# A windowed-attention block on one core: make_k and project ahead of turn 1, make_q and center2 ahead of attend 0, with two small moves beside it

## The chip, the cores and the metric

The program runs on one core of one Trainium2 chip. The time is the device time of an execution in microseconds (us), lower is better. The five engines are TensorE (PE), VectorE (DVE), ScalarE (ACT), GpSimd (POOL) and SyncE (SP, which here only moves data). Each works through its own list of instructions in order, and they meet only at semaphores.

## The reference, cut to what matters

One Swin block on x of shape (4, 32, 64, 64): windows of 8 x 8 positions, 4 heads of 8 channels, all in float32.

```python
xw = windows(x)                                     # (4*64, 64, 32)
h = layernorm(xw, ln1_g, ln1_b)
q, k, v = split(h @ qkv_w.T + qkv_b)                # 4 heads of 8
attn = softmax((q * 8 ** -0.5) @ k.T + bias)        # 64 x 64 for each window and head
o = (attn @ v) @ proj_w.T + proj_b
xw = xw + o
h = gelu(layernorm(xw, ln2_g, ln2_b) @ fc1_w.T + fc1_b)
out = xw + h @ fc2_w.T + fc2_b
```

## The kernel before

The 128 partitions hold the 4 images' 32 channels. The picture is cut into 8 stripes of 8 rows (512 positions, 8 windows for each image). Every engine's program is a loop over c = 0 to 9; pass c, called body c here, works on three stripes at once: the attention of stripe c, the first layernorm and q, k, v of stripe f = c + 1, and projection, residual and second layernorm of stripe p = c - 1. What comes first on an engine is fixed by the order of calls in that loop, written out by hand; no scheduler changes it. After the attention bodies the two MLP products of all stripes follow.

The attention of a stripe goes in two halves t = 0, 1 of four units each (a unit g is one image's 4 windows of that half), with these steps:

- PE `score(c, t)` (L678): q times masked k into the four PSUM banks S_PS[0..3], one for each image.
- DVE `add_bias` (L485) copies a bank with the bias added into s_sb, and `find_max` (L495) takes the row maximum; POOL `subtract_max` (L215) subtracts it.
- PE `turn(c, r)` (L694), r = 0 to 3, transposes two units into the banks T_PS[0] and T_PS[1]; ACT `exp_round(c, r)` (L260) takes the exponential into pt. Turn r + 1 waits until exp r has read the banks.
- PE `attend(c, t)` multiplies pt by v (L712) and by ones for the denominators (L719). For t = 0 both go to S_PS[1]. ACT `inv_den(c, t)` makes the inverse by Ln (L321) and Exp (L323), and DVE `divide(c, t)` (L515) multiplies it in. The next stripe's score writes all four banks and so waits for divide(c, 0), among four other semaphores.

For the next stripe: PE `center1` (L610), ACT `square1` (L267), PE `variance1` (L628), ACT `inv_std1` (L273, L275), DVE `norm1` (L503), then PE `make_k` and `make_q` (L604) and `make_v` (L653), and ACT `copy_k` (L285, with the head-masked copies at L290), `copy_q` (L298) and `copy_v` (L313); POOL `mask_keys` (L207) makes the other two masked copies. For the stripe before: PE `project` (L610), DVE `residual` (L521), PE `center2` (L610), DVE `keep2` (L526), ACT `square2` (L329), PE `variance2` (L604), ACT `log_var2` and `inv_std2` (L335, L339), POOL `norm2` (L221). project, center2 and variance2 all use the bank Y_PS. PE takes pairs of them together (make_k with project, make_q with center2, variance2 with center1), since they use different quarters of the array; their waits stand ahead of the pair.

The listings of the order below are of one engine each, without repeats of the same instruction.

## Time and profile before

| | us |
|---|---|
| median of 3 runs | 177.25 (176.6 to 177.63) |
| the profiled execution's own time | 178.3 |
| its span, first to last instruction | 176.6 |
| PE busy | 156.7 |
| ACT busy | 128.2 |
| DVE busy | 118.9 |
| POOL busy | 91.1 |

The span is what the trace shows; the rest of the execution's time lies around it. Body 0 begins at 15.73, body 7 at 124.65, and the MLP stage, with the largest part of the output transfers, runs from about 147 to the end. A busy engine is not yet the bound: what counts is which wait ends last in a stage.

### The profile page before, as it was taken

What the parts mean: (1) busy time and instruction counts of PE and PEld (TensorE: products, weight loads), DVE (VectorE), ACT (ScalarE), POOL (GpSimd) and SP (SyncE); (2) the same over time, 40 slices, a digit from 0 to 9 for tenths busy, and PEclk for the clock granted to TensorE, in tenths of its full rate; (3) what the DMA queues carried; (4) which work ended last, traced back from release to release, by engine and by line L of the source; (5) the groups of instructions that cost most, each with busy time, mean ns of one, the idle gap of its engine ahead of it and who ended that gap; (6) DMA issues with size and microseconds to landing.
All of it is one profiled execution on the core that took longest, in us unless ns stands there. A gap on an engine that the chain in (4) does not pass through costs nothing.

```text
span 176.6 us, 6351 instructions
## 1 busy us (share of the span) xinstructions
PE 156.7 (89%) x2688; PEld 86.7 (49%) x2688; DVE 118.9 (67%) x220; ACT 128.2 (73%) x180; POOL 91.1 (52%) x103
## 2 busy tenths in 40 slices
PE   7978699999999999999999999999999794749972
PEld 7535354764575556457555754664575350111210
DVE  4556996969777896979597787969788702303332
ACT  4344967759697798769687977878683459788991
POOL 7500658638584947657585848668587420020000
PEclk9999999999999999999999999999999999988999
DMA  2760000000000000000000000000000000101333
GB/s 75 222 206 0 4 2 4 4 0 4 6 4 0 4 0 4 6 2 4 4 4 0 4 4 2 4 4 4 2 4 4 0 4 0 59 0 59 123 119 119
DMA packets 3245, 4.71 MB, mean 27 GB/s; under 512 B 946, under 2 KB 1298, under 8 KB 3218
## 3 DMA queue, kind: packets, MB, share of 16 engines
q1 hardware_dynamic: 2840, 4.23, 7.1%
q8 instruction: 21, 0.34, 0.8%
q0 software_dynamic: 256, 0.07, 0.3%
q14 instruction: 6, 0.05, 0.1%
q10 hardware_dynamic: 122, 0.01, 0.1%
HBM read 2.21 MB, written 2.10 MB: 24 GB/s over the span
## 4 chain that ended last, share of the span: by engine, by line
PE 57%; ACT 26%; DVE 7%; issue 7%; ACTq 1%; POOLq 1%; DVEq 0%
PE ps L694 14%; ACT pt L260 11%; PE ps L604 9%; PE ps L712 7%; PE ps L678 7%; PE ps L719 5%; ACT hid L350 4%; DVE s_sb L485 4%; ACT v_blk L313 3%; PE ps L757 3%; PE ps L771 3%; PE ps L653 3%; PE ps L586 2%; ACT rstd L339 2%; PE ps L610 2%
## 5 line engine op out<-in xcount | busy, mean ns | idle before, releaser
L215 POOL TENSOR_TENSOR s_sb<-s_sb,mx 128x512 f32<-128x512 f32 x64 | 66.1, 1042 | 46.9 <-DVE mx L495 46.9
L485 DVE TENSOR_TENSOR s_sb<-ps,bias_t 128x512 f32<-128x512 f32 x64 | 43.7, 683 | 12.4 <-PE ps L678 12.4
L495 DVE TENSOR_REDUCE mx<-s_sb 128x8 f32<-128x512 f32 x64 | 43.9, 686 | 2.2
L260 ACT ACTIVATE pt<-ps 128x1024 f32<-128x1024 f32 x32 | 32.7, 1021 | 12.9 <-PE ps L694 12.7
L694 PEld LDWEIGHTS ps<-ident,s_sb 128*128 128x128 f32 x256 | 27.4, 140 | 22.5 <-issue 20.7
L694 PE MATMUL ps<-ident,s_sb 128*128 128x128 f32 x256 | 35.2, 279 | 2.1 <-ACT pt L260 1.4
L678 PE MATMUL ps<-k_m,q_sb 32*64 32x256 f32 x512 | 18.5, 386 | 2.4 <-DVE att L515 1.4
L712 PEld LDWEIGHTS ps<-pt,v_blk 128*32 128x32 f32 x1024 | 15.2, 110 | 9.7 <-ACT pt L260 9.2
L712 PE MATMUL ps<-pt,v_blk 128*32 128x64 f32 x1024 | 17.8, 221 | 1.3 <-ACT pt L260 0.3
L610 PE MATMUL ps<-x_sb,cent_m 64*64 64x512 f32 x64 | 18.0, 640 | 0.9 <-DVE x_sb L521 0.9
L350 ACT ACTIVATE hid<-ps,fb 128x512 f32<-128x512 f32 (+1 forms) x16 | 16.8, 1110 | 1.8 <-PE ps L757 1.8
L604 PE MATMUL ps<-h,wqk 64*64 64x512 f32 x64 | 17.0, 613 | 0.9 <-DVE h L503 0.9
L561 DVE SCALAR_TENSOR_TENSOR y_sb<-ps,vec,x_sb 128x512 f32<-128x512 f32 (+1 forms) x9 | 6.2, 691 | 16.9 <-PE ps L771 16.9
L221 POOL TENSOR_TENSOR h_sb<-h_sb,rstd 128x512 f32<-128x512 f32 x8 | 10.2, 1275 | 13.4 <-ACT rstd L339 13.4
L719 PE MATMUL ps<-pt,ones_h 128*32 128x256 f32 x256 | 16.8, 379 | 0.0
L515 DVE TENSOR_TENSOR att<-ps,den 128x256 f32<-128x256 f32 x16 | 6.7, 420 | 14.6 <-ACT den L323 14.6
L678 PEld LDWEIGHTS ps<-k_m,q_sb 32*64 32x64 f32 x512 | 10.6, 131 | 6.1 <-ACT q_sb L298 2.8
L757 PE MATMUL ps<-h_sb,f_s 32*128 32x512 f32 x64 | 9.9, 686 | 2.4 <-POOL h_sb L221 2.4
L207 POOL TENSOR_SCALAR k_m<-k_sb,hmask 128x512 f32<-128x512 f32 x14 | 9.5, 692 | 3.7 <-ACT k_sb L285 3.7
L653 PEld LDWEIGHTS ps<-wv,h 128*64 128x64 f32 x256 | 8.1, 138 | 5.7 <-issue 3.1
L771 PE MATMUL ps<-hid,f_st 128*32 128x512 f32 (+1 forms) x72 | 9.4, 607 | 1.6 <-ACT hid L350 1.6
L604 PE MATMUL ps<-sq,mean_m 64*64 64x512 f32 x32 | 8.6, 613 | 2.2 <-ACT sq L329 2.1
(92 smaller groups left out, 180.2 us busy)
## 6 DMA issues: line engine op xcount, KB each, us to landing
x_sb<-in_x_dram SPq DMA_DIRECT2D x8, 256.0 KB, 4.9
out_dram<-y_sb SPq DMA_DIRECT2D x7, 256.0 KB, 2.0
out_dram<-y_sb SPq DMA_DIRECT2D x2, 128.0 KB, 1.8
raw_b<-in_L_conv_rpb_dram POOLq DMA_DIRECT2D x8, 8.0 KB, 2.8
f_nat<-in_L_conv_fc_w_dram SPq DMA_DIRECT2D x2, 16.0 KB
w_nat<-in_L_conv_qkv_w_dram ACTq DMA_DIRECT2D x1, 12.0 KB
p_nat<-in_L_conv_proj_w_dram SPq DMA_DIRECT2D x1, 4.0 KB
vec_r<-in_L_conv_ln_g_dram ACTq DMA_DIRECT2D x1, 0.1 KB
```

The costliest lines, as they stand in the source:

```text
L215: pool.tensor_tensor(tile, tile, mx[:, n % 4, :].unsqueeze(2).to_broadcast([128, 2 * NH, NT]), ALU.subtract).then_inc(shifted, 1)
L260: act.activation(pt[:, n % 8:n % 8 + 2, :, :, :].rearrange("p u a k n -> p (u a k n)"), ps[:, 4:6, :].rearrange("p u n -> p (u n)"), ACT.E ...
L350: act.activation(hid[:, c % 2, images, :].rearrange("p g n -> p (g n)"), ps[:, banks, :].rearrange("p g n -> p (g n)"), ACT.Gelu, bias=fb1 ...
L485: dve.tensor_tensor(s_sb[:, n % NSB, :, :, :].rearrange("p a h m -> p a (h m)"), S_PS[g].rearrange("p (a k) -> p a k", a=2), bias_t[:, :, ...
L495: dve.reduce_max(mx[:, n % 4, :], s_sb[:, n % NSB, :, :, :].rearrange("p a h m -> p (a h) m"), AX.X)\
L604: ins = pe.matmul(out[r:r + 64, :], w[r:r + 64, r:r + 64], rhs[r:r + 64, :], start=True, stop=True, tile_position=(r, r))
L610: ins = pe.matmul(out[64 - r:128 - r, :], w[r:r + 64, r:r + 64], rhs[r:r + 64, :], start=True, stop=True, tile_position=(r, 64 - r))
L678: ins = pe.matmul(S_PS[g][NT * ab:NT * (ab + 1), 256 * pr:256 * (pr + 1)], q_sb[C * g:C * (g + 1), c % 2, NT * w:NT * (w + 1)], k_m[C * g: ...
L694: ins = pe.transpose(T_PS[u][:, 128 * i:128 * (i + 1)], s_sb[:, n % NSB, pr, 2 * hp:2 * hp + 2, :].rearrange("p h m -> p (h m)"), ident[:, :])
L712: ins = pe.matmul(OD_PS[t][C * g:C * (g + 1), NT * wl:NT * (wl + 1)], v_blk[:, c % 2, G * (4 * t + wl) + g, 32 * (1 - hp):32 * (2 - hp)], ...
L719: ins = pe.matmul(OD_PS[t][C * g:C * (g + 1), 256:512], ones_h[:, hp, :], pt[:, (4 * t + g) % 8, :, hp, :], start=(hp == 0), stop=(hp == 1 ...
L757: ins = pe.matmul(ps[:, first_bank(c) + g, :], f1_s[C * g:C * (g + 1), :], h2_sb[C * g:C * (g + 1), c, :], start=True, stop=True, tile_pos ...
```

## The change

Four things move.

1. PE: make_k and project, which stood behind turn 1, stand ahead of it, and attend 0, which stood ahead of make_q and center2, stands behind them. The same instructions are issued.
2. ACT: copy_k is split. Its plain copy stands between exp 0 and exp 1; the two head-masked copies, now `scale_k`, come after exp 1, then copy_q, and inv_den(c, 0) after that, where it stood ahead of copy_q.
3. DVE: residual comes after the first unit of the second half instead of after the second, and divide(c, 0) stands ahead of the last find_max instead of behind it.
4. First values: the v product of stripe 0 goes to T_PS[0] instead of S_PS[0] and no longer waits for the first variance; the first score waits for that variance's Ln instead of for the copy of v, and the first turn waits for the copy of v.

```diff
--- before.py
+++ after.py
@@ -283,6 +283,8 @@
                 if f >= 1:
                     act.wait_ge(k_masked, f)
                 act.activation(k_sb[:, :], X_PS, ACT.Identity, bias=bq[:, 1:2]).then_inc(k_copied, 1)
+
+            def scale_k(f):
                 if f >= 2:
                     act.wait_ge(scored, 8 * (f - 1))
                 if f >= 1:
@@ -309,7 +311,7 @@
 
                     dst = v_blk[r, f % 2, :, 16:48].rearrange("p w (k e) -> p w k e", e=16)
                     dst = dst[:, :, ::-1, HD * hh:HD * (hh + 1)]
-                    src = S_PS[1 if f else 0][r].rearrange("p (w k d) -> p w k d", k=2, d=HD)
+                    src = (S_PS[1] if f else T_PS[0])[r].rearrange("p (w k d) -> p w k d", k=2, d=HD)
                     ins = act.activation(dst, src, ACT.Copy)
                 ins.then_inc(v_copied, 1)
 
@@ -375,16 +377,18 @@
                     act.preload_act_table_set("natural_log_exp_and_others")
                 if there(c):
                     exp_round(c, 0)
-                    exp_round(c, 1)
                 if there(f):
                     copy_k(f)
                     if f == 0:
                         copy_q(f)
                         copy_v(f)
                 if there(c):
+                    exp_round(c, 1)
+                if f >= 1 and there(f):
+                    scale_k(f)
+                    copy_q(f)
+                if there(c):
                     inv_den(c, 0)
-                if f >= 1 and there(f):
-                    copy_q(f)
                 if there(p):
                     square2(p)
                 if there(c):
@@ -538,16 +542,18 @@
                 if there(p):
                     divide(p, 1)
                 if there(c):
-                    for g in range(2):
-                        add_bias(c, 1, g)
-                        find_max(c, 1, g)
+                    add_bias(c, 1, 0)
+                    find_max(c, 1, 0)
                 if there(p):
                     residual(p)
                 if there(c):
-                    for g in range(2, G):
-                        add_bias(c, 1, g)
-                        find_max(c, 1, g)
+                    add_bias(c, 1, 1)
+                    find_max(c, 1, 1)
+                    add_bias(c, 1, 2)
+                    find_max(c, 1, 2)
+                    add_bias(c, 1, 3)
                     divide(c, 0)
+                    find_max(c, 1, 3)
                 if there(p):
                     keep2(p)
                 if c == -1:
@@ -646,11 +652,9 @@
             def make_v(f):
                 if f >= 1:
                     pe.wait_ge(biased, unit_of(f, 0, 1) + 1)
-                else:
-                    pe.wait_ge(log1, 1)
                 for w in range(NW):
                     for hh in range(2):
-                        ins = pe.matmul(S_PS[1 if f else 0][NT * hh:NT * (hh + 1), NT * w:NT * (w + 1)], h1[:, f % 2, w, :],
+                        ins = pe.matmul((S_PS[1] if f else T_PS[0])[NT * hh:NT * (hh + 1), NT * w:NT * (w + 1)], h1[:, f % 2, w, :],
                                         wv[:, hh, :, :].rearrange("p k d -> p (k d)"), start=True, stop=True,
                                         tile_position=(0, NT * hh))
                 ins.then_inc(v_ready, 1)
@@ -663,7 +667,7 @@
                         pe.wait_ge(k_scaled, c)
                         pe.wait_ge(divided, 2 * (c - 1) + 1)
                     else:
-                        pe.wait_ge(v_copied, 1)
+                        pe.wait_ge(log1, 1)
                 else:
                     pe.wait_ge(v_copied, c + 1)
                     if there(c + 1):
@@ -688,6 +692,8 @@
                     pe.wait_ge(shifted, n + 1)
                     if n >= 2:
                         pe.wait_ge(expd, n - 1)
+                    else:
+                        pe.wait_ge(v_copied, 1)
                     for pr in range(2):
                         for hp in range(2):
                             i = 2 * pr + hp
@@ -812,17 +818,16 @@
                 if there(c):
                     turn(c, 0)
                     score(c, 1)
+                if there(f):
+                    wait_k(f)
+                if there(p):
+                    wait_project(p)
+                if there(f):
+                    make_k(f)
+                if there(p):
+                    project(p)
+                if there(c):
                     turn(c, 1)
-                if there(f):
-                    wait_k(f)
-                if there(p):
-                    wait_project(p)
-                if there(f):
-                    make_k(f)
-                if there(p):
-                    project(p)
-                if there(c):
-                    attend(c, 0)
                 if there(f):
                     wait_q(f)
                 if there(p):
@@ -834,6 +839,7 @@
                 if p == NCH - 1:
                     down(0, 4, slice(0, TC))
                 if there(c):
+                    attend(c, 0)
                     turn(c, 2)
 
             up(1)
```

PE, one body from its second score on (body 1), before:

```order
L678 MATMUL ps<-k_m,q_sb 64x256 x16
L694 MATMUL ps<-ident,s_sb 128x128 x8
L604 MATMUL ps<-h1,wqk 64x512 x2
L610 MATMUL ps<-att,wp 64x512 x2
L712 MATMUL ps<-pt,v_blk 32x64 x32
L719 MATMUL ps<-pt,ones_h 32x256 x8
L604 MATMUL ps<-h1,wqk 64x512 x2
L610 MATMUL ps<-x1_sb,cent_m 64x512 x2
L694 MATMUL ps<-ident,s_sb 128x128 x8
L678 MATMUL ps<-k_m,q_sb 64x256 x16
L604 MATMUL ps<-sq2,mean_m 64x512 x2
```

and now (L610 is make_k, make_q and variance2, L616 project, center2 and center1, L700 the turn, L718 and L725 attend, L682 the score):

```order
L682 MATMUL ps<-k_m,q_sb 64x256 x16
L610 MATMUL ps<-h1,wqk 64x512 x2
L616 MATMUL ps<-att,wp 64x512 x2
L700 MATMUL ps<-ident,s_sb 128x128 x8
L610 MATMUL ps<-h1,wqk 64x512 x2
L616 MATMUL ps<-x1_sb,cent_m 64x512 x2
L718 MATMUL ps<-pt,v_blk 32x64 x32
L725 MATMUL ps<-pt,ones_h 32x256 x8
L700 MATMUL ps<-ident,s_sb 128x128 x8
L682 MATMUL ps<-k_m,q_sb 64x256 x16
L610 MATMUL ps<-sq2,mean_m 64x512 x2
```

Between attend's products and the next score there is now a turn alone, where make_q, center2 and the turn stood.

DVE, the same body from the first add_bias of its second half, before (L485 add_bias, L495 find_max, L521 residual, L515 divide, L526 keep2):

```order
L485 TENSOR_TENSOR s_sb<-ps,bias_t 128x512
L495 TENSOR_REDUCE mx<-s_sb 128x8
L485 TENSOR_TENSOR s_sb<-ps,bias_t 128x512
L495 TENSOR_REDUCE mx<-s_sb 128x8
L521 SCALAR_TENSOR_TENSOR x1_sb<-ps,bq,x_sb 128x512
L485 TENSOR_TENSOR s_sb<-ps,bias_t 128x512
L495 TENSOR_REDUCE mx<-s_sb 128x8
L485 TENSOR_TENSOR s_sb<-ps,bias_t 128x512
L495 TENSOR_REDUCE mx<-s_sb 128x8
L515 TENSOR_TENSOR att<-ps,den 128x4x8x8
L526 COPY h2_sb<-ps 128x512
```

and now (L489, L499, L525, L519, L530 in the same order):

```order
L489 TENSOR_TENSOR s_sb<-ps,bias_t 128x512
L499 TENSOR_REDUCE mx<-s_sb 128x8
L525 SCALAR_TENSOR_TENSOR x1_sb<-ps,bq,x_sb 128x512
L489 TENSOR_TENSOR s_sb<-ps,bias_t 128x512
L499 TENSOR_REDUCE mx<-s_sb 128x8
L489 TENSOR_TENSOR s_sb<-ps,bias_t 128x512
L499 TENSOR_REDUCE mx<-s_sb 128x8
L489 TENSOR_TENSOR s_sb<-ps,bias_t 128x512
L519 TENSOR_TENSOR att<-ps,den 128x4x8x8
L499 TENSOR_REDUCE mx<-s_sb 128x8
L530 COPY h2_sb<-ps 128x512
```

The residual moved up by one pair; the divide moved ahead of the last find_max, so that find_max and keep2 stand behind it.

## Rows read from the trace of the kernel before

**Rows 1.** Page, part 1: busy us, share of the span, instructions of each engine.
```profile
PE 156.7 (89%) x2688; PEld 86.7 (49%) x2688; DVE 118.9 (67%) x220; ACT 128.2 (73%) x180; POOL 91.1 (52%) x103
```

**Rows 2.** Five bodies as one stretch: length, busy us (instructions) of PE, PEld, DVE, ACT, POOL, granted clock, DMA share, GB/s.
```profile
44.98:124.65 79.67, 76.72 (x1571) 46.85 (x1571) 65.36 (x106) 64.15 (x100) 54.10 (x56) 1.00 0.01 3
```

**Rows 3.** Timeline of PE: start, us, operation, count, idle before and its releaser.
```profile
95.02 1.09 PE L694 MATMUL ps<-ident,s_sb 128*128 128x128 f32 x8
...
100.90 1.12 PE L678 MATMUL ps<-k_m,q_sb 32*64 32x256 f32 x32
102.22 1.07 PE L694 MATMUL ps<-ident,s_sb 128*128 128x128 f32 x8 [0.21 <-ACT pt L260]
103.22 0.65 PE L604 MATMUL ps<-h,wqk 64*64 64x512 f32 x2
...
104.45 1.10 PE L712 MATMUL ps<-pt,v_blk 128*32 128x64 f32 x64
...
106.35 0.65 PE L604 MATMUL ps<-h,wqk 64*64 64x512 f32 x2
...
107.37 1.09 PE L694 MATMUL ps<-ident,s_sb 128*128 128x128 f32 x8
108.69 1.33 PE L678 MATMUL ps<-k_m,q_sb 32*64 32x256 f32 x32 [0.23 <-DVE att L515]
```

**Rows 4.** Timeline of DVE, the same body.
```profile
101.20 0.42 DVE L515 TENSOR_TENSOR att<-ps,den 128x256 f32<-128x256 f32 x1 [1.22 <-ACT den L323]
102.08 0.69 DVE L485 TENSOR_TENSOR s_sb<-ps,bias_t 128x512 f32<-128x512 f32 x1 [0.45 <-PE ps L678]
...
104.72 0.74 DVE L521 SCALAR_TENSOR_TENSOR x_sb<-ps,bq,x_sb 128x512 f32<-128x512 f32 x1
...
107.42 0.69 DVE L495 TENSOR_REDUCE mx<-s_sb 128x8 f32<-128x512 f32 x1
108.02 0.41 DVE L515 TENSOR_TENSOR att<-ps,den 128x256 f32<-128x256 f32 x1
108.35 0.68 DVE L526 COPY h_sb<-ps 128x512 f32<-128x512 f32 x1
```

**Rows 5.** Opening: timeline of PE, then of DVE.
```profile
14.58 0.38 PE L600 MATMUL ps<-vec,f_t 32*128 32x1 f32 x2
15.73 1.12 PE L678 MATMUL ps<-k_m,q_sb 32*64 32x256 f32 x32 [0.77 <-ACT v_blk L313]
...
13.23 1.68 DVE L465 TENSOR_SCALAR k_m<-k_sb,hmask 128x512 f32<-128x512 f32 x4 [0.26 <-ACT k_sb L285]
```

**Rows 6.** Bodies 0 and 1: timeline of DVE, then of PE.
```profile
22.25 0.68 DVE L503 TENSOR_TENSOR h<-ps,rstd 128x512 f32<-128x512 f32 x1
...
29.26 1.12 PE L678 MATMUL ps<-k_m,q_sb 32*64 32x256 f32 x32
...
37.19 1.12 PE L678 MATMUL ps<-k_m,q_sb 32*64 32x256 f32 x32
```

**Rows 7.** Timeline of ACT, the body of rows 3.
```profile
100.68 0.42 ACT L323 ACTIVATE den<-den 128x256 f32<-128x256 f32 x1
101.05 1.02 ACT L260 ACTIVATE pt<-ps 128x1024 f32<-128x1024 f32 x1
103.37 1.02 ACT L260 ACTIVATE pt<-ps 128x1024 f32<-128x1024 f32 x1 [1.29 <-PE ps L694]
...
106.48 0.38 ACT L321 ACTIVATE den<-ps 128x256 f32<-128x256 f32 x1
106.90 0.42 ACT L323 ACTIVATE den<-den 128x256 f32<-128x256 f32 x1
...
109.06 0.63 ACT L329 ACTIVATE sq<-h_sb 128x512 f32<-128x512 f32 x1 [0.90 <-DVE h_sb L526]
109.60 1.01 ACT L260 ACTIVATE pt<-ps 128x1024 f32<-128x1024 f32 x1
```

**Rows 8.** Timeline of PE behind the last body.
```profile
140.74 1.08 PE L604 MATMUL ps<-sq,mean_m 64*64 64x512 f32 x4 [1.30 <-ACT sq L329]
```

More of the change, by code:

```diff
@@ L814, in _ @@
                     score(c, 1)
-                    turn(c, 1)
                 if there(f):
@@ L824, in _ @@
                 if there(c):
-                    attend(c, 0)
+                    turn(c, 1)
                 if there(f):
```

## The prediction

> **What bounds the kernel now.** I read the page first. TensorE (PE) is busy 156.7 of 176.6 us, 89%, where ScalarE (ACT) and VectorE (DVE) have 128.2 and 118.9 [rows 1]. The stretch of five whole bodies, 44.98 to 124.65, takes 79.67 us, 15.93 us a body, of which PE is busy 76.72, 15.34 a body, at clock 1.00 [rows 2]. So a body is bound by PE's list of work, and about 0.6 us of it is waits. The timeline of one body tells which. PE idles 0.21 us before turn 1 of stripe c, because exp 0 ends late. It waits before attend 0 too: make_k and project start at 103.22 and take as long as make_q and center2 do (106.35 to 107.37, 1.02), so they would be through at 104.24, and attend starts at 104.45, after exp 1 (103.37 + 1.02). It idles 0.23 before score 0 of the next stripe, released by the divide, which starts at 108.02 [rows 3, 4, 7]. (A PE row's end lies 0.07 to 0.09 beyond the start of the next, as 102.22 + 1.07 against 103.22; steps below go from start to start.) The three ask for different things: the first two for other work in front of them, the third for an earlier divide.
>
> **Opening.** The first score, at 15.73, sat idle 0.77 us for the copy of v, while PE had finished its last setup product, started at 14.58 and 0.38 long, at 14.96. Without that wait its last releaser is the masking of the keys, 13.23 + 1.68 = 14.91 [rows 5]. The v matmuls now go to a bank that only turns use, and turn 0 of stripe 0 stands after DVE's add, find_max and GpSimd's subtraction, long after v is copied, so the new wait there costs nothing; were that cover gone it would give the gain back. The score's own release latency is between 0.06 us (PE free at 14.96 and 14.91 + 0.06) and the 0.26 between the end of the divide (108.02 + 0.41) and 108.69 [rows 3, 4]. The score starts between 14.97 and 15.17; I take 15.05, and everything behind it shifts by **-0.68** us (bounds -0.56 and -0.76).
>
> **Body 0, the first with the new order.** make_k now stands before turn 1. It needs h1 of the next stripe, which DVE makes from 22.25 for 0.68, so make_k starts at 23.00, old time [rows 6]. Turn 1 then starts at 24.02 and lasts 1.09, exp 1 runs 25.16 to 26.18, make_q hides beside it, and attend 0 starts at 26.24. Now the new tail: only turn 2 stands between attend 0 and the next score. Call the start of attend 0 A. The denominator's Ln, which waits for attend's sums, starts 2.03 after A (104.45 to 106.48), its Exp 0.42 later (106.90), and lasts 0.42 [rows 3, 7]. The divide starts about 0.10 us after that, which is the lag of the row where DVE had been idle for it (101.20, after an Exp that began at 100.68), takes 0.41 and releases the score 0.26 later [rows 3, 4, 7]. The sum is 2.03 + 0.42 + 0.42 + 0.10 + 0.41 + 0.26 = 3.64: **the next score starts at A + 3.64**. PE itself has only attend (1.90 to the next start) and turn 2 (1.02), 2.92. For body 0 that is 29.88, against 29.26 [rows 6]: **+0.62**.
>
> **Body 1.** Score 0 to score 1 is the same list as before, 7.93 us (29.26 to 37.19). make_k follows 1.04 later (a score row's 1.12 less the overlap), turn 1 1.02 after that, at 39.87. center2 needs the residual: add_bias of unit 0 starts 1.18 after score 1 (100.90 to 102.08), the residual follows one add_bias and find_max pair later, 1.32 (two pairs lie between 102.08 and 104.72), and takes 0.74, so 3.24 + 0.06 after score 1: 41.12. PE itself would be free at 40.87, so 0.25 us of new idle. Attend 0 is 1.02 later, 42.14, and the next score at 45.78 where it was at 44.98 [rows 2, 3, 4, 6]. The body is 15.90 long against 15.72: **+0.18**.
>
> **Bodies 2 to 6, the term that decides.** From here variance2 stands behind the score, and it needs keep2 and square2 of the stripe before. The diff puts the divide ahead of the last find_max. That is good while the divide is ready when DVE gets there, as now. But with attend 0 moved behind make_q it isn't: DVE reaches the divide some 0.8 us too early (make_q's residual wait puts the last add_bias at 12.20 + 3.24 - 0.08 + 2 x 1.32 = A' + 1.5, done at A' + 2.2) and stands, with the last find_max and keep2 queued behind it. The divide starts at A + 2.97. find_max follows 0.33 later (the step 108.02 to 108.35), keep2 0.60 after that (107.42 to 108.02) and takes 0.68, ending at A + 4.58. square2 starts 0.03 later and takes 0.63, and variance2 can start at A + 5.30 [rows 4, 7]. PE would be free for it at A + 3.64 + 1.04, so it idles 0.6 us more. Exp 2 stands behind square2 on ACT by 0.54 and lasts 1.01; turn 3 needs it 0.15 after its end (as turn 1 came 0.15 after exp 0, 101.05 + 1.02), A + 6.31, just when variance2 and center1 (1.02) are through, A + 6.32. From turn 3 to score 1 the list is unchanged, 5.88 (95.02 to 100.90): A + 12.20. Then make_k at 13.24; turn 1 at 14.26; make_q at 12.20 + 3.30 = 15.50, the residual again; the next attend 0 at A + 16.53 [rows 3, 6]. Exp 1 would let it go at 14.26 + 1.09 + 0.05 + 1.02 + 0.06 = 16.48 [rows 3, 7], so it no longer ends a wait. k_scale and the copy of q run on ACT beside attend and end before the Ln is wanted. **A body takes 16.53 us instead of 15.93**, and five take 82.65 instead of 79.67: **+2.98**. The vanished waits are paid back twice: 0.7 us before the score, 0.6 before variance2.
>
> Here the row of DVE and a rule part ways. The find_max at 107.42 lasts 0.69, and the next instruction starts after 0.60 [rows 4]. The Trainium skill (VectorE: DVE Perf Modes, "The DRAIN you can't avoid") says that after each operation a drain of its length less 266 ns stands before the next; by that, find_max would hold keep2 back by 0.69 + 0.42 = 1.11 us, 0.51 more a body, and six bodies would put the time 3.1 us above mine, at 184.7. The same page lets an operation that is not held start earlier, and this row is of that kind. I keep 0.60.
>
> **Body 7 and the tail.** No next stripe, so make_k, make_q and center1 fall away. Before, the variance2 that follows it came 16.09 us after this body's score 0 (124.65 to 140.74), with 1.30 us of waiting in front of it for divide, keep2 and square2 [rows 2, 8]. In the new order, counted from the score, which stands at 128.43: variance2 + 1.66 (5.30 - 3.64), turn 3 + 2.68, score 1 + 7.71 (the 5.88 less variance1, which I estimate at 0.85, between half and all of make_q and center2), project + 8.75, turn 1 + 9.77, center2 + 11.01 (the residual again), attend 0 + 12.04, and variance2 at 12.04 + 5.30 = 17.34. **+1.25**. With variance1 at 0.5 or 1.02 the term is 1.6 or 1.1. Behind it the program is the same, so the shift is carried to the end.
>
> **Sum.** -0.68 + 0.62 + 0.18 + 2.98 + 1.25 = +4.35 us. The span goes from 176.6 to 181.0 and the profiled execution's own time from 178.3 to 182.6; that execution stands 1.05 us above the median of the runs, 177.25, and since the difference is what I have, the median becomes 177.25 + 4.35 = **181.6 us**.
>
> **Rivals.** (1) *Faster: the filled gaps count and the divide does not bind.* The mechanism is the score's release after attend 0. It decides at one point: if the path from A to the score, 3.64 us, fitted into attend and turn 2, 2.92. Then a body loses its three waits, 0.65 us, less the 0.25 of the residual: -0.4 in six bodies and -0.68, **174.2**. For it: those two gaps are real [rows 3], and PE is the bound [rows 1]. Against: every term of the path has its row, and the code makes the score wait for this divide. The Trainium skill (Perfetto Trace Analysis, "Matmul Optimizations") wants matmuls back to back in batches, which speaks for the change as it is meant. Chance 0.05. (2) *No change: keep2 keeps up.* If variance2 were not late, a body would be 16.53 - 0.62 = 15.91, as now, and the last one +0.63: -0.68 + 0.62 + 0.18 + 0.63 = +0.75; with the residual's wait hidden too, seven times 0.25 less. **176.3 to 178.0**. It decides almost at once: today square2 ends at 109.06 + 0.63 = 109.69 and the score could make room at 109.73. Against: keep2 moves from 0.34 before the score to 0.26 after it [rows 3, 4, 7]. Chance 0.05. (3) *Slower still: the links are longer.* Exp 2 and turn 3 meet within 0.01 us, so any lag of DVE or ACT between the divide and exp 2 beyond those of the rows goes straight into the body; the find_max at its full 0.69 and two lags of 0.15 in place of 0.03 and 0.06 make 0.3, lags of 0.26 as the divide's make 0.5. 0.3 to 0.5 us a body on six gives 1.8 to 3 us more, **183.4 to 184.6**. Against: the links come from rows with the same neighbours. The drain that the Trainium skill states would act here too, at 184.7. Chance 0.13. (4) *The change does not do what it says*, its waits being so placed that attend 0 is not delayed: the listing of the order excludes it for PE. Chance 0.01, no change.
>
> **How the numbers follow.** The forecast has 0.76. Its own range is 180.6 to 182.8: five links of 0.05 in six bodies make 1.0, the opening 0.1, and the median of three runs moves by half a us. The range I give reaches to the longer links and halfway to rival 2: **180.0 to 183.8**. 0.5% is 0.9 us, about what a measurement of this kernel can tell from no change. Slower by more: 0.76 + 0.13 = 0.89. Within: rivals 2 and 4, 0.06. Faster: 0.05.
>
> **What would show it.** In the new profile: score 0 released by the divide with 0.6 to 0.7 us idle in each body; variance2 released by square2 with about 0.6; DVE idle about 0.8 us before the divide, released by the denominator's Exp; no idle left before turn 1; attend 0 no longer released by exp 1 with a gap; score-to-score 16.5 us; first score at 15.05. If score-to-score is 15.9, keep2 was hidden and rival 2 holds; if 15.5, the divide was. If the first score isn't earlier, another setup wait stands behind v's.

## The result and the profile after

| | before | changed |
|---|---|---|
| median of 4 executions each, us | 177.22 | 184.33 (182.89 to 185.02) |
| ratio | | 1.038 [1.034, 1.043] |
| the profiled execution's own time | 178.3 | 182.89 |
| its span | 176.6 | 181.1 |

The kernel became 7.1 us slower. The forecast was 181.6 us with a range of 180.0 to 183.8: the direction and the mechanism hold, the size does not, and the time lies 0.5 us above the range. Note that the profiled execution of the changed kernel is the lowest of its four, 1.4 us under their median, while that of the kernel before was 1.1 us above its own. The two spans differ by 4.5 us only. Ratios use fast executions alone; of all those below one was slow, 187.56 us in e1, and without it e1's median is 184.31.

The body with the move, as PE's timeline of the changed kernel shows it (start, us, operation, count, idle before and its releaser; L682 score, L610 make_q or variance2, L616 center2 or center1, L700 turn, L718 and L725 attend):

```profile
103.11 1.12 PE L682 MATMUL ps<-k_m,q_sb 32*64 32x256 f32 x32
104.16 0.65 PE L610 MATMUL ps<-h,wqk 64*64 64x512 f32 x2
...
105.18 1.09 PE L700 MATMUL ps<-ident,s_sb 128*128 128x128 f32 x8
106.51 0.65 PE L610 MATMUL ps<-h,wqk 64*64 64x512 f32 x2 [0.23 <-DVE x_sb L525]
...
107.53 1.10 PE L718 MATMUL ps<-pt,v_blk 128*32 128x64 f32 x64
...
109.42 1.10 PE L700 MATMUL ps<-ident,s_sb 128*128 128x128 f32 x8
111.16 1.12 PE L682 MATMUL ps<-k_m,q_sb 32*64 32x256 f32 x32 [0.64 <-DVE att L519]
112.90 0.65 PE L610 MATMUL ps<-sq,mean_m 64*64 64x512 f32 x2 [0.62 <-ACT sq L331]
```

Against [rows 3]: the idle before turn 1 and before attend 0 is gone, as meant. In its place PE stands 0.23 us for the residual, 0.64 for the divide (0.23 before) and 0.62 for square2, where the next body followed at once. The reason for the last two is on DVE in the same body (L489 add_bias, L519 divide, L499 find_max, L530 keep2):

```profile
108.92 0.68 DVE L489 TENSOR_TENSOR s_sb<-ps,bias_t 128x512 f32<-128x512 f32 x1
110.48 0.42 DVE L519 TENSOR_TENSOR att<-ps,den 128x256 f32<-128x256 f32 x1 [0.88 <-issue]
110.82 0.68 DVE L499 TENSOR_REDUCE mx<-s_sb 128x8 f32<-128x512 f32 x1
111.42 0.68 DVE L530 COPY h_sb<-ps 128x512 f32<-128x512 f32 x1
```

DVE is through with its last add_bias at 109.60 and stands 0.88 us. find_max, which could run then, and keep2 are queued behind the divide. In [rows 4] the same divide followed find_max without a gap. The profile names no releaser for this wait ("issue"); by the code it is for the inverse of the denominator, whose last step on ACT ends at 110.39, 0.09 us before the divide starts:

```profile
109.56 0.38 ACT L323 ACTIVATE den<-ps 128x256 f32<-128x256 f32 x1 [0.26 <-PE ps L725]
109.97 0.42 ACT L325 ACTIVATE den<-den 128x256 f32<-128x256 f32 x1
```

Ln starts 2.03 us after attend, 107.53, as in [rows 3, 7]; only attend itself has moved. The copies that the change put ahead of Ln on ACT do not delay it here: ACT stands 0.26 us for attend's sums before Ln. The move on ACT was not run by itself. The five bodies as one stretch, as [rows 2], with the same PE work and 3.9 us more length:

```profile
44.25:127.86 83.61, 76.46 (x1571) 46.69 (x1571) 65.46 (x106) 63.82 (x100) 54.40 (x55) 1.00 0.01 3
```

That is 16.72 us a body, against 15.93. Behind body 7 the wait for square2 grew from 1.30 [rows 8] to 2.30 us:

```profile
145.28 1.08 PE L610 MATMUL ps<-sq,mean_m 64*64 64x512 f32 x4 [2.30 <-ACT sq L331]
```

### The profile page after: what moved, and what is told of

Same layout as the page of the kernel before. It is cut to its first block, busy times and chain, and to the rows that moved or that the text cites. A ratio compares the mean times of both kernels' runs of the same rounds, so it can differ in the third digit from the quotient of the medians.

```text
span 181.1 us, 6353 instructions
## 1 busy us (share of the span) xinstructions
PE 155.3 (86%) x2688; PEld 86.6 (48%) x2688; DVE 118.8 (66%) x220; ACT 127.7 (70%) x180; POOL 91.5 (51%) x103
## 4 chain that ended last, share of the span: by engine, by line
PE 60%; DVE 17%; ACT 12%; issue 8%; ACTq 1%; POOLq 1%; DVEq 0%
PE ps L610 10%; PE ps L718 9%; PE ps L700 9%; PE ps L725 8%; PE ps L682 6%; DVE mx L499 5%; PE ps L657 4%; DVE s_sb L489 4%; ACT hid L352 4%; PE ps L634 3%; PE ps L763 3%; DVE x_sb L525 3%; ACT sq L331 3%; PE ps L777 3%; DVE h_sb L530 2%
## 5 line engine op out<-in xcount | busy, mean ns | idle before, releaser
L489 DVE TENSOR_TENSOR s_sb<-ps,bias_t 128x512 f32<-128x512 f32 x64 | 43.8, 684 | 6.9 <-PE ps L682 6.9
L499 DVE TENSOR_REDUCE mx<-s_sb 128x8 f32<-128x512 f32 x64 | 43.9, 685 | 2.0
L700 PEld LDWEIGHTS ps<-ident,s_sb 128*128 128x128 f32 x256 | 27.4, 140 | 20.8 <-issue 14.2
L700 PE MATMUL ps<-ident,s_sb 128*128 128x128 f32 x256 | 35.2, 280 | 0.6 <-POOL s_sb L215 0.6
L519 DVE TENSOR_TENSOR att<-ps,den 128x256 f32<-128x256 f32 x16 | 6.8, 425 | 25.9 <-ACT den L325 19.8
L682 PE MATMUL ps<-k_m,q_sb 32*64 32x256 f32 x512 | 18.4, 386 | 4.8 <-DVE att L519 4.5
L610 PE MATMUL ps<-h,wqk 64*64 64x512 f32 x64 | 17.0, 610 | 2.4 <-DVE x_sb L525 1.4
L718 PEld LDWEIGHTS ps<-pt,v_blk 128*32 128x32 f32 x1024 | 15.0, 110 | 8.3 <-ACT pt L260 7.9
L616 PE MATMUL ps<-x_sb,cent_m 64*64 64x512 f32 x64 | 17.2, 615 | 1.0 <-DVE x_sb L525 1.0
L718 PE MATMUL ps<-pt,v_blk 128*32 128x64 f32 x1024 | 17.6, 220 | 0.3 <-ACT pt L260 0.2
L725 PE MATMUL ps<-pt,ones_h 128*32 128x256 f32 x256 | 16.7, 379 | 0.0
L682 PEld LDWEIGHTS ps<-k_m,q_sb 32*64 32x64 f32 x512 | 10.6, 131 | 8.6 <-issue 7.6
L610 PE MATMUL ps<-sq,mean_m 64*64 64x512 f32 x32 | 8.6, 610 | 6.4 <-ACT sq L331 6.4
L331 ACT ACTIVATE sq<-h_sb 128x512 f32<-128x512 f32 x8 | 5.0, 630 | 12.3 <-DVE h_sb L530 12.3
L285 ACT ACTIVATE k_sb<-ps,bq 128x512 f32<-128x512 f32 x8 | 5.5, 694 | 9.4 <-PE ps L610 9.4
```

The source lines that it names most:

```text
L489: dve.tensor_tensor(s_sb[:, n % NSB, :, :, :].rearrange("p a h m -> p a (h m)"), S_PS[g].rearrange("p (a k) -> p a k", a=2), bias_t[:, :, ...
L499: dve.reduce_max(mx[:, n % 4, :], s_sb[:, n % NSB, :, :, :].rearrange("p a h m -> p (a h) m"), AX.X)\
L610: ins = pe.matmul(out[r:r + 64, :], w[r:r + 64, r:r + 64], rhs[r:r + 64, :], start=True, stop=True, tile_position=(r, r))
L616: ins = pe.matmul(out[64 - r:128 - r, :], w[r:r + 64, r:r + 64], rhs[r:r + 64, :], start=True, stop=True, tile_position=(r, 64 - r))
L682: ins = pe.matmul(S_PS[g][NT * ab:NT * (ab + 1), 256 * pr:256 * (pr + 1)], q_sb[C * g:C * (g + 1), c % 2, NT * w:NT * (w + 1)], k_m[C * g: ...
L700: ins = pe.transpose(T_PS[u][:, 128 * i:128 * (i + 1)], s_sb[:, n % NSB, pr, 2 * hp:2 * hp + 2, :].rearrange("p h m -> p (h m)"), ident[:, :])
```

## Why 7.1 us in the median and 4.5 in the spans

The opening differs by more than the change. The first centring product, whose instructions and place are those of before, took 1.85 us before and 1.07 here. Why is not shown: the granted clock of the stretch from 5 to 7 us reads 1.00, the level of 2.4 GHz, in both. PE's timeline of the opening in the kernel before:

```profile
5.37 1.85 PE L610 MATMUL ps<-x_sb,cent_m 64*64 64x512 f32 x4
```

And in the changed kernel, with the last setup product (L606) and the first score (L682):

```profile
5.21 1.07 PE L616 MATMUL ps<-x_sb,cent_m 64*64 64x512 f32 x4
...
13.66 0.38 PE L606 MATMUL ps<-vec,f_t 32*128 32x1 f32 x2
14.08 1.12 PE L682 MATMUL ps<-k_m,q_sb 32*64 32x256 f32 x32
```

It does not go with the change: the changed kernel itself, profiled twice more below (e1 and e9), takes 1.52 us for this product both times, and e3 and e12, which are one program, take 1.44 and 1.07. So 0.92 us of the 1.65 by which the first score came earlier (15.73 to 14.08) is chance. The change's own part is the distance from the last setup product to the score: 1.15 before [rows 5], 0.42 now, 0.73 us. That distance is not quite fixed either: in the 13 profiles of kernels with the new first values it is 0.42 to 0.54 us and once, in e6, 0.91. From the first score to the variance2 behind body 7 it is 125.01 us before (15.73 to 140.74) and 131.20 after (14.08 to 145.28), +6.19. So the change costs 6.19 - 0.73 = **5.5 us** in its order of work, and the span hides 0.9 of it. What is left of the median's 7.1, some 1.6 us, does not show in this pair of traces at all; it is looked for below.

## Experiments

**e1, the changed kernel again.** No edit.

> The changed kernel again, nothing edited. Its profiled execution had a span of 181.1 us, 4.5 above the kernel before, while the medians differ by 7.1. Theory A (the queue behind the divide explains the whole difference, the rest is where the opening happened to fall): the profiled body is 16.7 us again, and the median of the executions is 184.0 to 184.7. Theory B (the new waits of PE also lower its granted clock in most executions): executions of this kernel show a mean clock near 0.98 and a span 1.5 to 2 us above 181.1, those of the kernel before stay at 0.990.

Measured: median 184.36 (182.64 to 187.56), ratio 1.040 [1.031, 1.048]. The profiled execution, of 184.41 us, has a mean clock of 0.981 where the first had 0.991. Its five bodies take 83.66 us (44.86 to 128.52), so the loop is the same to 0.05 us, and the clock there is 1.00. The difference lies behind the wait of 2.29 us, in PE's timeline of e1:

```profile
145.95 1.70 PE L610 MATMUL ps<-sq,mean_m 64*64 64x512 f32 x4 [2.29 <-ACT sq L331]
147.58 1.97 PE L700 MATMUL ps<-ident,s_sb 128*128 128x128 f32 x8
```

The granted clock of the stretch from 145.9 to 149.4 is 0.55, that is nearly all of it at 1.2 GHz (length, busy us of PE, PEld, DVE, ACT, POOL, clock, DMA share, GB/s):

```profile
145.90:149.40 3.50, 3.45 (x12) 1.76 (x12) 0.00 (x0) 1.59 (x2) 0.00 (x0) 0.55 0.00 0
```

The same variance2 took 1.08 us in the first profile, with the same wait of 2.30 in front of it, and the turn behind it 1.09. So the wait that the change lengthened is one behind which the clock sometimes falls. Theory B has a place, and the spans give its size in this trace. Of the 1.6 us that e1's span (182.7) lies above the first profile's (181.1), 0.61 lie in the opening (first score at 14.69 in place of 14.08), 0.06 between the first score and this variance2, and 0.93 behind it (36.75 us to the end in place of 35.82). The products behind the later wait of 2.4 us, before up(1), took 1.14 us in e1 and 2.04 in the first profile: a second stretch at the lower clock stands there in the first profile, while in e1 it stands at 157.0 to 160.7 (granted clock 0.61).

**e2, find_max back ahead of the divide.**

```diff
                     add_bias(c, 1, 3)
-                    divide(c, 0)
                     find_max(c, 1, 3)
+                    divide(c, 0)
```

> The changed kernel with the last find_max of a stripe put back ahead of the divide; everything else as changed. Theory A: find_max then runs in the time that DVE stands waiting for the denominator, keep2 and square2 come 0.6 us earlier, and a body falls from 16.7 to 16.1 us; six bodies give -3.6, so about 180.7 us. The wait of PE before the score (0.65) stays, the one before variance2 (0.6) goes. Rival (the order on DVE doesn't matter, the late attend alone costs the time): 184.3 us, variance2 as late as before.

Measured: 179.34 (178.78 to 180.26), ratio 1.013 [1.006, 1.021], 5.0 us below the changed kernel, where 3.6 were worked out. The five bodies as one stretch of e2:

```profile
45.15:125.80 80.65, 76.16 (x1571) 46.56 (x1571) 65.78 (x106) 63.79 (x100) 54.31 (x56) 1.00 0.01 3
```

16.13 us a body, 0.59 less. PE's timeline of e2 at the head of a body:

```profile
93.59 1.12 PE L682 MATMUL ps<-k_m,q_sb 32*64 32x256 f32 x32 [0.64 <-DVE att L519]
94.74 0.65 PE L610 MATMUL ps<-sq,mean_m 64*64 64x512 f32 x2
```

DVE's timeline of e2 at the same place:

```profile
92.06 0.69 DVE L499 TENSOR_REDUCE mx<-s_sb 128x8 f32<-128x512 f32 x1
92.91 0.42 DVE L519 TENSOR_TENSOR att<-ps,den 128x256 f32<-128x256 f32 x1 [0.17 <-ACT den L325]
93.25 0.68 DVE L530 COPY h_sb<-ps 128x512 f32<-128x512 f32 x1
```

The wait for the divide is untouched at 0.64, the one for square2 is all but gone (variance2 starts 1.15 us after the score, where 1.05 is the distance in e4 below), and DVE's own wait fell from 0.88 to 0.17. Two lines in a different order on an engine that is only 66% busy are 5 us: this part of theory A is shown. From the first score to the variance2 behind body 7 it is 127.06 us in e2 (14.98 to 142.04) against 131.20, so the traces show 4.1 of the 5.0; 1.2 of them lie in body 7 alone (16.24 against 17.42), where the last wait is 1.71 us in place of 2.30 and the working had 0.6. The other 0.9 us of the medians the two traces do not show. The kernel before needs 125.01 us for the same way, so some 2 us of the change's 6.19 remain in e2: there attend 0 is still late and the score still waits.

**e3, the first values alone, on the kernel before.** The three lines of the diff on make_v, copy_v and the waits of the first score and turn.

> The kernel before with only the first values changed (v of stripe 0 into T_PS[0], the first score no longer behind its copy). If the wait for v was the last one there: the first score starts about 0.7 us earlier against the setup product ahead of it (0.3 us after its start and not 1.15), and the time is 0.7 us lower, 176.5. If another wait takes its place: no change, 177.2.

Measured: 176.70 against 176.58, ratio 1.000 [0.996, 1.003]. The trace shows the edit at work, the first score 0.42 us after the last setup product, but the median leaves open whether it comes through. With more executions:

> The kernel before with the first values alone, in five rounds, since e3 left it open: its trace has the first score 0.42 us after the last setup product and not 1.15, its median was the same. If the 0.73 us come through to the end: 0.5 to 0.8 us below the kernel before, ratio 0.996. If something later takes them back: ratio 1.000.

Measured: 176.80 against 177.51, ratio 0.997 [0.993, 1.000]. The two intervals overlap between 0.996 and 1.000; 0.73 us is 0.996. The gain of the trace fits both, and neither shows it by itself.

**e4, divide and keep2 first, with attend 0 where it was.** On the kernel before with e3's values:

```diff
-                    for g in range(2, G):
-                        add_bias(c, 1, g)
-                        find_max(c, 1, g)
+                    add_bias(c, 1, 2)
+                    find_max(c, 1, 2)
+                    add_bias(c, 1, 3)
                     divide(c, 0)
                 if there(p):
                     keep2(p)
+                if there(c):
+                    find_max(c, 1, 3)
```

> The kernel before with the first values of e3, and on DVE the divide and then keep2 ahead of the last find_max; PE's and ACT's order and the residual stay as before. With attend 0 where it was the denominator is ready when DVE gets there. Theory A (divide, keep2 and square2 are what PE waits for at the head of a body, and the place of attend 0 decides whether they can be early): the wait of 0.23 before the score goes and variance2 follows the score at once, a body 15.5 to 15.6 us and not 15.93, the time 173.7 to 175.0. Rival (a body is PE's list of 15.3 us and other waits fill in): as e3, 176.5.

Measured: 173.26 (172.69 to 174.51) against 176.58, ratio 0.981 [0.974, 0.988]. It beats both kernels, and comes out 0.4 us below the range that was worked out. The five bodies of e4 as one stretch:

```profile
42.98:120.17 77.19, 75.45 (x1571) 45.66 (x1570) 65.41 (x107) 64.01 (x100) 54.38 (x56) 1.00 0.01 3
```

PE's timeline of e4 at the head of a body:

```profile
89.29 1.12 PE L678 MATMUL ps<-k_m,q_sb 32*64 32x256 f32 x32
90.34 0.65 PE L606 MATMUL ps<-sq,mean_m 64*64 64x512 f32 x2
```

And DVE's (L515 divide, L526 keep2, L495 find_max):

```profile
88.31 0.42 DVE L515 TENSOR_TENSOR att<-ps,den 128x256 f32<-128x256 f32 x1
88.65 0.68 DVE L526 COPY h_sb<-ps 128x512 f32<-128x512 f32 x1
89.25 0.68 DVE L495 TENSOR_REDUCE mx<-s_sb 128x8 f32<-128x512 f32 x1
```

15.44 us a body; neither the score nor variance2 waits. The divide is ahead of find_max as in the changed kernel, and DVE doesn't stand for it, since attend 0 began 2.95 us before, with make_q and center2 behind it. The same idea, an early divide, gains or loses by where attend stands.

**e5 and e6, spare products in the waits of the tail.** Products of zeros into an unused bank, 7, 4, 2, 2 and 7 of them, in the waits that PE has from body 8 to up(1); they are work added, with no part in the result. e5 is on the changed kernel, e6 on e4.

```diff
+            def fill(n):
+                pe.wait_ge(k_copied, NCH)
+                pe.wait_ge(k_scaled, NCH - 1)
+                for _ in range(n):
+                    pe.matmul(X_PS[:, 0:128], blank[:, :], blank[:, :], start=True, stop=True)
...
+                if p == NCH - 1:
+                    fill(7)
+                if p == NCH:
+                    fill(2)
                 if there(p - 1):
                     wait_variance2(p - 1)
...
```

> The changed kernel with 22 spare 128 x 128 products of zeros put into the waits that PE has from body 8 on (7 before the last variance2 but one, where it stands idle 2.3 us, 4 before project, 2 before center2, 2 before the last variance2, 7 before up(1), idle 2.4 us); they write the bank of the centred x, which nobody uses any more, and take no part in the result. Each takes some 0.28 us, so they fit the waits within 0.4 us. In the profiled executions so far the granted clock falls to half somewhere behind these waits, for some 3.4 us once or twice. Theory B (the new wait of 2.3 us costs clock, and that is part of the 7 us): no stretch at half clock, mean clock above 0.995, median 181.0 to 182.5 and the executions closer together. Theory A alone: clock and median as before this edit, 184.4, or some tenths higher where the products do not quite fit.

> The kernel of e4 (173.26 us) with the same spare products. Theory B: mean clock above 0.995 and about 1.5 us less, 171.5 to 172.3, since the wait of 2.4 us before up(1) is in this kernel too. Otherwise 173.3 or a little more.

Measured: e5 182.75 (182.52 to 183.93), e6 173.99 (173.68 to 174.40). On the changed kernel the products bring 1.6 us against e1, but the intervals of the two ratios overlap (1.034 [1.026, 1.042] and 1.040 [1.031, 1.048]), and the mean clock of e5's executions, 0.992 to 0.996, is not above 0.995 as theory B expected. In e5's profile it is 1.00 behind the filled waits and 0.88 in the last 12 us. On e4 they bring nothing: the ratios to the kernel before are 0.983 with them and 0.981 without, although the mean clock was 1.000 (0.990 in e4's profile). There the wait for square2 behind body 7 is only 0.70 us and the products of 1.73 us overran it by some 1.0; variance2 was 1.5 us later than in e4 (135.66, here 137.15), 0.7 us of which lie in the opening already. So no gain of 1.5 us from a clock kept up everywhere shows here; a smaller one could be hidden by the overrun and the opening. That e4's stretch at 1.2 GHz lies beside work of ACT, which would make it free, fits this and was not tried apart from the overrun.

**e9, e10, e11: the changed kernel, e5's products, and one wait alone, with more executions.**

> The changed kernel once more, in five rounds, as the partner of e10 and e11 on the same chip. In the trace of e1 the products behind the wait of 2.3 us in body 8 ran at half clock and the way from that variance2 to up(1) took 18.3 us, in the first profile of the changed kernel and in that of the kernel before 16.1. Theory B (that wait decides, and most executions fall into the lower clock there): median 184.0 to 184.8. Theory A: the same, and e10 and e11 the same as this.

> The kernel of e5 (all waits from body 8 on filled with spare products) in five rounds. Theory B: 182.5 to 183.2, 1.2 to 1.8 us below e9 with intervals that don't overlap. Theory A: as e9, within 0.3 us.

> The changed kernel with spare products in one wait alone, the one of 2.3 us before the variance2 of body 8, which the change made 1.0 us longer (7 products, no part in the result). If this wait decides for the clock: at least two thirds of what e10 gains, so 183.0 to 183.4. If the later waits (2.4 us before up(1), as in the kernel before) decide: as e9.

Measured: e9 183.61 (182.44 to 185.10), e10 182.76 (182.23 to 183.51), e11 183.20 (182.46 to 183.96). The intervals of the ratios overlap: 1.037 [1.030, 1.044], 1.032 [1.027, 1.037], 1.034 [1.029, 1.039]. By what was expected that is a miss for either theory: e9 lies below the 184.0 to 184.8 of both, e10 gains 0.85 us on it and not 1.2 to 1.8, and e11 keeps half of that gain, not two thirds. The single executions say more than the medians. The changed kernel has been executed 14 times in all: five between 182.4 and 183.0, nine at 184.2 or more, none between. Their mean clocks fall into the same two groups, 0.991 in each of the five and 0.975 to 0.982 in the nine. The kernel before has both too, in other shares: of its 37 executions beside these experiments, 26 stand at 0.990 or more and 11 at 0.977 to 0.985. With products in the new wait (e5, e10, e11, 16 executions) all lie between 182.2 and 184.0, and e11's clocks are 0.986 to 0.991. The three profiles of the changed kernel fit the two groups: 182.89 us with variance2 at full clock behind the wait, 184.41 and 184.26 at half clock. In e9's profile the way from that variance2 to the end is 0.79 us longer than in the first profile, in e1's 0.93. In e11 the wait left is 0.73 us and the products behind it run at full clock, as PE's timeline shows:

```profile
146.22 1.08 PE L616 MATMUL ps<-sq,mean_m 64*64 64x512 f32 x4 [0.73 <-ACT sq L331]
147.22 1.09 PE L706 MATMUL ps<-ident,s_sb 128*128 128x128 f32 x8
```

The median of the 14 is 184.3, that of the ten of e5 and e10 182.8: 1.5 us, as much as was missing. That filling the new wait takes the upper group away is shown. That the lower clock behind it is the whole of the 1.6 us is not: the two traces put 0.8 to 0.9 us there and another 0.6 in the opening, where the centring product took 1.52 us in place of 1.07, and whether the two go together no run shows. e11's profile has the full clock behind the wait and that slow opening (1.55), and is the slowest of its six, 183.96. The medians of one kernel also move from one measurement to the next, 183.61 to 184.36 for the changed kernel and 176.58 to 177.51 for the one before.

**e7, the two small moves without those on PE and ACT.** The kernel before with the diff's edits on DVE (residual after one unit, divide ahead of the last find_max) and the first values.

> The kernel before with the two small moves of the change as the diff has them (first values; residual one pair up and divide ahead of the last find_max), without the moves on PE and ACT. The residual then stands ahead of the second add_bias while the project that it waits for ends 0.9 us later, and attend 0 waits for that add_bias: DVE stands about 0.95 us a body, attend 0 starts 1.2 us late, a body 16.9 to 17.2 us, the time 183 to 185. If DVE's order is harmless without the moves on PE: 176 to 177.

Measured: 186.29 (186.22 to 186.78), ratio 1.053 [1.047, 1.059]: slower than the whole change, and 1.3 us more than the upper end of what was worked out. Five bodies take 86.48 us (44.56 to 131.04), 17.30 each. DVE's timeline of e7 (L521 residual, L485 add_bias):

```profile
91.08 0.75 DVE L521 SCALAR_TENSOR_TENSOR x_sb<-ps,bq,x_sb 128x512 f32<-128x512 f32 x1 [0.91 <-PE ps L612]
91.75 0.68 DVE L485 TENSOR_TENSOR s_sb<-ps,bias_t 128x512 f32<-128x512 f32 x1
```

PE's timeline of e7 at attend 0:

```profile
92.57 1.10 PE L714 MATMUL ps<-pt,v_blk 128*32 128x64 f32 x64 [1.59 <-DVE s_sb L485]
```

The residual waits for project, the second add_bias stands behind it, and attend 0 waits 1.59 us for that add_bias to free the bank. So the small moves are not small by themselves; the residual's place needs project ahead of turn 1.

**e8, make_k and project ahead of turn 1, attend 0 where it was.** On e4; ACT's plain copy of k stands between exp 0 and exp 1 and its masked copies behind exp 1, as in the change. On PE:

```diff
                     score(c, 1)
-                    turn(c, 1)
                 if there(f):
                     wait_k(f)
...
                 if there(p):
                     project(p)
                 if there(c):
+                    turn(c, 1)
                     attend(c, 0)
```

> The kernel of e4 with make_k and project ahead of turn 1 (and copy_k between exp 0 and exp 1, the head-masked copies behind exp 1) as in the change, but attend 0 where it was, ahead of make_q and center2. It separates the two halves of the move on PE. If the filled wait before turn 1 counts by itself: a body 0.2 us shorter, 172. My working: attend 0 then stands right behind turn 1 and waits for exp 1, 0.05 + 1.02 + 0.06 = 1.13 us of idle in place of 0.21 + 0.21, a body 0.7 us longer, about 178.

Measured, in a single execution: 178.70 us, 81.07 us for five bodies (44.44 to 125.51), 16.21 each against 15.44 in e4. PE's timeline of e8 at turn 1 (L701) and attend 0 (L719):

```profile
86.89 1.09 PE L701 MATMUL ps<-ident,s_sb 128*128 128x128 f32 x8
89.14 1.10 PE L719 MATMUL ps<-pt,v_blk 128*32 128x64 f32 x64 [1.16 <-ACT pt L260]
```

The wait of 0.2 before turn 1 became one of 1.16 before attend 0: once turn 1 is late, exp 1 is what attend waits for, and make_q and center2 are what would cover it. That cover is what delays attend in the change. So the first half of the move on PE doesn't pay by itself, while both together put make_q and center2, 1.02 us of PE's work, ahead of attend 0, where before they stood behind it and in the time that its divide took. The other half alone, attend 0 behind make_q with make_k and project where they were, was not run.

## Where the prediction was right and where it failed

- **Opening**, -0.68 forecast: 0.73 in the distance from the setup product to the score. The first score was forecast at 15.05 and came at 14.08, since the centring product was shorter in that execution.
- **Bodies 0 and 1**: from the first score to that of body 2 it is 30.17 us (14.08 to 44.25), worked out 30.05 with the opening taken away. Good to 0.12.
- **The next score at A + 3.64**: 107.53 to 111.16, 3.63. The idle time before it 0.64, forecast 0.6 to 0.7.
- **Bodies 2 to 6**, 16.53 forecast, 16.72 measured; +2.98 became +3.94. The step that was mis-sized is the lag of a pair of PE products behind its releaser. I took 0.06 us behind square2 and behind the residual. The residual ended at 105.62 + 0.74 = 106.36 and make_q began at 106.51, 0.15 later; variance2 came 0.14 behind square2 (95.44 + 0.63 to 96.21). Both lie on the path of every body, 0.08 to 0.09 each. The order, the waits and what ends them were as forecast. The rows, of DVE, ACT and PE of the changed kernel:

```profile
105.62 0.74 DVE L525 SCALAR_TENSOR_TENSOR x_sb<-ps,bq,x_sb 128x512 f32<-128x512 f32 x1
...
95.44 0.63 ACT L331 ACTIVATE sq<-h_sb 128x512 f32<-128x512 f32 x1 [1.74 <-DVE h_sb L530]
...
96.21 0.65 PE L610 MATMUL ps<-sq,mean_m 64*64 64x512 f32 x2 [0.62 <-ACT sq L331]
```

In body 7, where a product has no partner, 0.06 was right: variance2 alone starts 0.06 us behind square2 (128.82 + 0.63 to 129.51), center2 alone 0.06 behind the residual (138.19 + 0.74 to 138.99), and both stand 1.65 and 3.30 us after their scores, against 1.66 and 3.30 forecast. In the bodies it is 1.74 and 3.39. The longer lag goes with the pair.

- **Body 7**, 17.34 forecast, 17.42 measured (127.86 to 145.28).
- **Sum for the order of work**: -0.68 + 0.62 + 0.18 + 2.98 + 1.25 = 4.35 forecast, 5.5 measured. That is 1.1 of the 2.7 us that the median lies above the forecast, 1.0 of it in bodies 2 to 6 and nearly all of that these lags.
- **The time from the sum.** Here the step "since the difference is what I have, the median becomes 177.25 + 4.35" failed. The difference was worked out as if the granted clock behaved alike in both kernels. I had the wait behind body 7 at 1.30 us in the rows and my own working made it longer, to 2.2 us, and neither the sum nor a rival had a price for what PE's clock does behind a longer wait. The kernel before had the rows to price it with, its PE idle 2.43 us before up(1) and the products there at 1.87 us in place of 1.14:

```profile
153.30 1.14 PE L757 MATMUL ps<-h_sb,f_s 32*128 32x512 f32 x8
156.86 1.87 PE L757 MATMUL ps<-h_sb,f_s 32*128 32x512 f32 x8 [2.43 <-POOL h_sb L221]
```

With the 1.1 us of the lags alone the time would have been 182.7 and inside the range; the other 1.6 took it out. Of them the two traces put 0.8 to 0.9 us behind the longer wait, and the rest, openings among it, stays open.

- **Agreement of the spans was luck.** 181.0 forecast, 181.1 measured: the opening's 0.9 us offset the lags.
- **The range.** "Five links of 0.05 in six bodies" are 1.5 us and not 1.0. With 1.5 its upper end would have been some 183.3, and still below the result.
- **Rival 1** (faster, the divide does not bind) fell on its deciding point. The wait before the score is 0.64 in the changed kernel and zero in e4, where attend 0 stands early. **Rival 2** (keep2 keeps up) fell likewise, variance2 waits 0.62; e2 is the kernel in which it nearly holds, 16.13 us a body. **Rival 3** (longer links) was half right: two links of 0.14 to 0.15, 0.17 us a body and not 0.3 to 0.5. That the median, 184.33, lies in its range of 183.4 to 184.6 is luck: the links made 1.1 us and the rest came from elsewhere.
- **The drain** of a VectorE operation, as the Trainium skill states it (VectorE: DVE Perf Modes, "The DRAIN you can't avoid"), would have held keep2 1.11 us behind find_max. The row shows 0.60 (110.82 to 111.42), so the trace disagrees with that rule taken by itself and agrees with the exception that the prediction took. Its 184.7 us lies near the result without being its cause.

## What to carry to other kernels

A gap on the bound engine is filled at the cost of whatever is moved behind the filler: before moving, follow the moved work to the next thing that waits for it, and compare that path with the work that still stands in front of that wait (here 3.64 us against 2.92). On an engine that works in order, an instruction put ahead of others for an early result must be ready when its turn comes; otherwise it holds back what stands behind it, and two lines are worth 5 us here (e2). And a difference between two profiled executions is not yet one of the medians: compare stretch by stretch with the clock beside it, and give each longer wait of TensorE a possible price in clock.

## What the hardware showed beyond that

- Behind the same wait of 2.3 us the same products ran at 2.4 GHz in one execution and at 1.2 GHz in two (variance2 1.08, and 1.70 and 1.65 us), and the times fall into two groups 1.3 us or more apart.
- The mean clock alone does not give the time: with products in its waits the changed kernel's median came down by 1.6 and 0.85 us (e5 against e1, e10 against e9; mean clock of the profiles 0.992 and 0.993), while e6, at 1.000, was no faster than e4 at 0.990, with products that overran their wait.
- The first centring product took from 1.07 to 1.85 us in executions of kernels whose programs are alike up to there, which moves everything behind it by as much. The granted clock of that stretch reads 1.00 in the profiles of the slowest and of the fastest.
- PE started 0.05 to 0.06 us behind its releaser where a product of this kind stood alone (after the 1.30 us wait of [rows 8], the 2.30 us wait, and in body 7), and 0.14 to 0.15 us behind it in the bodies, where make_q and center2 follow the residual and variance2 and center1 follow square2 as pairs. In these rows the length of the wait makes no difference; no run changed the pairing by itself.
